# A fused attention and feed-forward kernel: the row maxima of a batch are turned by VectorE in 32x32 blocks instead of by TensorE

## The reference, cut to what matters

```
attn = einsum('bhqd,bhkd->bhqk', q, k) / sqrt(8) + slope[h] * -|i - j|
attn = softmax(attn, axis=-1)
x = layernorm(x + (attn @ v) @ wo.T + bo)
h = silu(x @ w1.T * s1) * (x @ w2.T * s2)
h = gelu(h @ h1.T * s) ; h = gelu(h @ h2.T * s)
x = layernorm(x + h @ w3.T * s3)
```

## Time and profile before

| | us |
|---|---|
| median of 3 runs | 811.47 (810.13 to 813.06) |
| profiled execution | 810.1 |
| its span, first to last instruction | 808.3 |
| busy TensorE / VectorE / ScalarE / GpSimd | 769.6 / 627.9 / 613.5 / 312.0 |

### The profile page before, as it was taken

How to read it: one execution, slowest core, us unless ns; L and a number is a source line. 1 busy time by engine, 2 the same in 40 slices (tenths; PEclk the granted TensorE clock), 3 DMA queues, 4 the chain that set the end, 5 groups by cost and what they waited for, 6 DMA issues and landing times.

```text
span 808.3 us, 26861 instructions
## 1 busy us (share of the span) xinstructions
PE 769.6 (95%) x10370; PEld 557.6 (69%) x10370; DVE 627.9 (78%) x1298; ACT 613.5 (76%) x1099; POOL 312.0 (39%) x488
## 2 busy tenths in 40 slices
PE   3899999999999999999998799999999999999994
PEld 2566666666666666666665578888888888888873
DVE  4789899899989999999993556777777766666764
ACT  3588788788888888888877767777777777777762
POOL 3447878787765657566543200000000000000001
PEclk7599999999999999999999999999999999999997
DMA  6565665656456464564521011111111111101001
GB/s 182 148 176 148 172 187 165 188 152 180 150 172 178 131 172 145 173 173 135 167 66 46 22 34 27 39 40 39 39 39 35 30 39 39 39 26 40 24 16 53
DMA packets 107341, 81.37 MB, mean 101 GB/s; under 512 B 11168, under 2 KB 94112, under 8 KB 107232
## 3 DMA queue, kind: packets, MB, share of 16 engines
q1 hardware_dynamic: 105632, 76.59, 33.3%
q0 software_dynamic: 880, 2.88, 1.3%
q10 hardware_dynamic: 720, 0.36, 0.1%
HBM read 45.72 MB, written 33.55 MB: 98 GB/s over the span
## 4 chain that ended last, share of the span: by engine, by line
PE 91%; DVE 2%; ACT 2%; DMA 2%; issue 1%; POOL 1%; SPq 0%; POOLq 0%; ACTq 0%; DVEq 0%
PE ps_b L947 17%; PE ps_b L950 17%; PE ps_o L524 15%; PE ps_a L465 11%; PE ps_b L473 6%; PE ps_b L580 4%; PE ps_a L950 3%; PE ps_a L947 3%; PE ps_a L549 2%; PE ps_a L480 2%; PE ps_b L541 2%; PE ps_a L563 2%; PE ps_b L480 2%; PE ps_b L571 1%; PE ps_b L535 1%
## 5 line engine op out<-in xcount | busy, mean ns | idle before, releaser
L759 DVE TENSOR_REDUCE neg_sb<-ps_a 128x2 f32<-128x512 f32 x512 | 324.6, 681 | 39.8 <-PE ps_a L480 32.6
L653 ACT ACTIVATE probs<-ps_b 128x512 f32<-128x512 f32 x512 | 281.5, 591 | 57.2 <-PE ps_b L480 57.0
L465 PE MATMUL ps_a<-qk_stack 52*64 52x256 bf16 x2048 | 177.3, 281 | 11.1 <-DMA qk_stack<-qk_scratch 8.2
L473 PE MATMUL ps_b<-qk_stack 54*64 54x256 bf16 x2048 | 172.4, 276 | 1.1 <-ACT probs L653 0.9
L1042 ACT ACTIVATE gelu_f<-ps_b,sc 128x512 f32<-128x512 f32 x128 | 88.3, 690 | 76.3 <-PE ps_b L950 68.7
L465 PEld LDWEIGHTS ps_a<-qk_stack 52*64 52x64 bf16 x2048 | 82.2, 108 | 84.4 <-DVE neg_sb L759 61.4
L524 PE MATMUL ps_o<-probs,v_aug 128*32 128x256 f32 x2048 | 137.5, 385 | 0.0
L1152 POOL TENSOR_SCALAR vareps_f<-meanvar_f 128x4 f32<-128x4 f32 x16 | 9.9, 618 | 319.2 <-DVE meanvar_f L1138 319.2
L480 PE MATMUL ps_a<-corner_sb,eye_sb 64*64 64x128 bf16 x1024 | 116.0, 222 | 0.3 <-issue 0.3
L480 PE MATMUL ps_b<-corner_sb,eye_sb 64*64 64x128 bf16 x1024 | 114.3, 218 | 0.2 <-issue 0.2
L947 PE MATMUL ps_b<-g1h,h_hi 128*128 128x512 f32 x256 | 101.6, 397 | 1.4 <-DVE g1l L1114 1.4
(11 more groups left out here) (112 smaller groups left out, 1429.9 us busy)
## 6 DMA issues: line engine op xcount, KB each, us to landing
qk_stack<-qk_scratch SPq DMA_DIRECT2D x128, 192.0 KB, 3.4
qk_scratch<-qk_sb SPq DMA_DIRECT2D x64, 192.0 KB, 3.0
qk_scratch<-qk_sb SPq DMA_DIRECT2D x96, 128.0 KB, 3.0
xT_sb<-in_xT SPq DMA_DIRECT2D x32, 128.0 KB, 3.5
x_sb<-in_x SPq DMA_DIRECT2D x32, 128.0 KB, 3.5
x_scratch<-x_sb SPq DMA_DIRECT2D x32, 128.0 KB, 3.4
x_in<-x_scratch SPq DMA_DIRECT2D x32, 128.0 KB, 2.1
x_res<-x_scratch SPq DMA_DIRECT2D x32, 128.0 KB, 2.1
```

The costliest lines, as they stand in the source:

```text
L465: pe.matmul(ps[side * TILE:(side + 1) * TILE, qb * SEQ:(qb + 1) * SEQ], q_stack[i][rows_of, j, at:at + TILE], k_stack[i][rows_of, j, :], s ...
L473: pe.matmul(ps[side * TILE:(side + 1) * TILE, kb * SEQ:(kb + 1) * SEQ], k_stack[i][rows_of, j, at:at + TILE], q_stack[i][rows_of, j, :], s ...
L653: nc.scalar.activation(probs[:, h % HALF, :], ps_b[b_bank(t, k)][:], ACT.Exp, scale=slope[h]).then_inc(exp_done, 1)
L759: nc.vector.tensor_reduce(negmax[:, h_a // HALF, h_a % GROUPS, h_a % HALF // GROUPS, :], ps_a[a_bank(t, k)][:].rearrange("p (b k) -> p b k ...
```

## The change

The turn of the maxima goes from TensorE to VectorE, which transposes blocks of 32x32 numbers only. `neg_sb` is now 128x32 (all 16 heads, two blocks of queries each), and `max_f` is 32x128. Behind the reduction of head 15, VectorE waits for all 16 reductions of the batch and writes `max_f` in four instructions, one for each 32 partitions. `turn_max` on TensorE, `copy_max` on ScalarE and their bank uses are gone. GpSimd splits all heads at once, and two transfers lay them in place of four. The first product runs 9 slots ahead in place of 4. In `AT`, `turn norm` goes from slot 8 to 9, `pv 1` from 10 to 9 and `qk` from 13 to 12. On ScalarE the copy of `o_sb` goes from behind slot 3 to behind slot 2 and `copy_oT` from slot 9 to 10. On VectorE `sum_stats` goes from slot 11 to 13.

```diff
-AT = {"v": 1, "wo": 1, "pv 3": 4, "max 0": 6, "turn o": 6, "pv 0": 6, "turn norm": 8, "pv 1": 10, "qk": 13, "max 1": 13, "pv 2": 15}
-AHEAD = 4
+AT = {"v": 1, "wo": 1, "pv 3": 4, "turn o": 6, "pv 0": 6, "turn norm": 9, "pv 1": 9, "qk": 12, "pv 2": 15}
+AHEAD = 9
-B_USES = [... for n in ("v", "max 0", "turn norm", "qk", "max 1") ...]
+B_USES = [... for n in ("v", "turn norm", "qk") ...]
...
-        neg_sb = sb("neg_sb", [P, 2, P])
+        neg_sb = sb("neg_sb", [P, BLK * HEADS])
-        max_f = [sb(f"max_f{i}", [BLK * HALF, P]) for i in range(2)]
+        max_f = sb("max_f", [BLK * HEADS, P])
...
 (SyncE)
-                if live(t, BATCH):
-                    max_rows(t, s, 1)
...
-                if live(t + 1, BATCH) and t >= 0:
-                    max_rows(t + 1, (s + 1) % STACKS, 0)
+                if live(t + 1, BATCH):
+                    max_rows(t + 1, (s + 1) % STACKS)
...
 (TensorE)
-                    if k % HALF == 0:
-                        wait(pe, m_landed[k // HALF], (t + 1) * MPARTS * DMA)
+                    if k == 0:
+                        wait(pe, m_landed, (t + 1) * MPARTS * DMA)
-                    if k == (3 if t < 0 else AT["max 0"]) and live(t + 1, BATCH):
-                        turn_max(t, 0)
-                    if k == AT["max 1"] and live(t + 1, BATCH):
-                        turn_max(t, 1)
...
 (ScalarE)
-                    if k == 3 and live(t - 1, BATCH):
+                    if k == 2 and live(t - 1, BATCH):
                         ...  (copy of o_sb)
-                    if k == 3 and live(t + 1, BATCH):
-                        copy_max(t, 0)
-                    if k == 9 and live(t - 1, BATCH - 1):
+                    if k == 10 and live(t - 1, BATCH - 1):
                         copy_oT(t)
-                    if k == 14 and live(t + 1, BATCH):
-                        copy_max(t, 1)
...
 (VectorE)
+            def turn_max(b):
+                wait(dve, max_done, (b + 1) * HEADS)
+                wait(dve, m_split, b)
+                for n in range(QUADS):
+                    quad = slice(n * SQUARE, (n + 1) * SQUARE)
+                    nc.vector.transpose(max_f[:, quad], neg_sb[quad, :]).then_inc(m_turned, 1)
...
-                        if h_a % HALF == 0:
-                            wait(dve, mT_done, b_a * 2 + h_a // HALF - 1)
+                        if h_a == 0:
+                            wait(dve, m_turned, b_a * QUADS)
                         ...  (the reduction)
+                        if h_a == HEADS - 1:
+                            turn_max(b_a)
-                    if k == 11 and live(t - 2, BATCH):
+                    if k == 13 and live(t - 2, BATCH):
                         sum_stats(t, par)
                     if k == 6 and live(t - 1, BATCH):
                         normalise(t)
...
 (GpSimd)
-                if live(t, BATCH):
-                    split_max(t, 1)
-                if t == -1:
-                    split_max(0, 0)
                 if live(t + 3, BATCH) and t + 3 > 0:
                     split_qk(t + 3, qk_sb[1 - par])
-                if live(t + 1, BATCH) and t >= 0:
-                    split_max(t + 1, 0)
+                if live(t + 1, BATCH):
+                    split_max(t + 1)
```

More of the change, by code:

```diff
@@ L73 @@
 SPILLS = 5
+SQUARE = 32
 XT_BUFS = 6
+QUADS = P // SQUARE
 def slopes():
@@ L93, in wait_apart @@
         eng.sem_inc(passed, 1)
-AT = {"v": 1, "wo": 1, "pv 3": 4, "max 0": 6, "turn o": 6, "pv 0": 6, "turn norm": 8, "pv 1": 10, "qk": 13, "max 1": 13, "pv 2": 15}
-AHEAD = 4
+AT = {"v": 1, "wo": 1, "pv 3": 4, "turn o": 6, "pv 0": 6, "turn norm": 9, "pv 1": 9, "qk": 12, "pv 2": 15}
+AHEAD = 9
 STACKS = 4
 A_USES = [use for k in range(HEADS) for use in (k, *(n for n in ("wo", "turn o") if AT[n] == k))]
-B_USES = [use for k in range(HEADS) for use in (k, *(n for n in ("v", "max 0", "turn norm", "qk", "max 1") if AT[n] == k))]
+B_USES = [use for k in range(HEADS) for use in (k, *(n for n in ("v", "turn norm", "qk") if AT[n] == k))]
 A_BANKS, B_BANKS = 3, 4
@@ L143, in b_batch @@
 def b_batch(t, use):
-    return t + {"v": 0, "max 0": 1, "max 1": 1, "turn norm": -1, "qk": 4}[use] if isinstance(use, str) else t
+    return t + {"v": 0, "turn norm": -1, "qk": 4}[use] if isinstance(use, str) else t
 def last_use(t, use, uses, banks, batch, first):
@@ L270, in attention @@
         xb_sb = [sb(f"xb_sb{i}", [P, BLK, D]) for i in range(2)]
-        neg_sb = sb("neg_sb", [P, 2, P])
-        negmax = neg_sb[:, :, 0:BLK * HALF].rearrange("p n (g h a) -> p n g h a", g=GROUPS, h=HH)
-        max_f = [sb(f"max_f{i}", [BLK * HALF, P]) for i in range(2)]
-        mrow = [sb(f"mrow{i}", [BLK * HALF, MPARTS, P], BF16) for i in range(2)]
+        neg_sb = sb("neg_sb", [P, BLK * HEADS])
+        negmax = neg_sb.rearrange("p (g h a) -> p g h a", g=GROUPS, h=HG)
+        max_f = sb("max_f", [BLK * HEADS, P])
+        mrow = sb("mrow", [BLK * HEADS, MPARTS, P], BF16)
         o_sb = sb("o_sb", [P, 2, SEQ])
@@ L300, in attention @@
         scores_a, max_done = sem("scores_a"), sem("max_done")
-        mT_done, m_copied, m_first, m_split = sem("mT_done"), sem("m_copied"), sem("m_first"), sem("m_split")
-        m_landed = [sem(f"m_landed{i}") for i in range(2)]
+        m_turned, m_first, m_split, m_landed = sem("m_turned"), sem("m_first"), sem("m_split"), sem("m_landed")
         scores_b, exp_done = sem("scores_b"), sem("exp_done")
@@ L308, in attention @@
         bn_done, xb_done = sem("bn_done"), sem("xb_done")
-        neg_set = sem("neg_set")
         ones_set, lo_marked, lo_counted = sem("ones_set"), sem("lo_marked"), sem("lo_counted")
@@ L454, in take_b @@
                         wait(pe, qk_copied, b + 1)
-                    elif isinstance(before[1], str):
-                        wait(pe, m_copied, b * 2 + int(before[1][-1]) + 1)
                     else:
@@ L528, in pv @@
                 mm.then_inc(pv_done, 1)
[L530 to L535, removed]
             def project_v(t):
@@ L625, in _ @@
         def _(act):
[L626 to L629, removed]
-                                     ACT.Copy).then_inc(m_copied, 1)
             def copy_oT(t):
@@ L816, in split_piece, with split_max @@
                 nc.gpsimd.tensor_tensor(lo, raw_piece(n), hi.bitcast(F32), ALU.subtract).then_inc(raw_split, 1)
-            def split_max(b, hf):
-                wait(pool, m_copied, b * 2 + hf + 1)
-                wait(pool, m_landed[hf], b * MPARTS * DMA)
-                nc.gpsimd.tensor_copy(mrow[hf][:, 0, :], max_f[hf][:]).then_inc(m_first, 1)
-                wait(pool, m_first, b * 2 + hf + 1)
-                nc.gpsimd.tensor_tensor(mrow[hf][:, 1, :], max_f[hf][:], mrow[hf][:, 0, :], ALU.subtract).then_inc(m_split, 1)
+            def split_max(b):
+                wait(pool, m_turned, (b + 1) * QUADS)
+                wait(pool, m_landed, b * MPARTS * DMA)
+                nc.gpsimd.tensor_copy(mrow[:, 0, :], max_f[:]).then_inc(m_first, 1)
+                wait(pool, m_first, b + 1)
+                nc.gpsimd.tensor_tensor(mrow[:, 1, :], max_f[:], mrow[:, 0, :], ALU.subtract).then_inc(m_split, 1)
             def split_qk(b, parts):
```

14 lines of the change are left out of this document (5 added, 9 removed).

## The result

The changed kernel takes 888.16 us (887.05 to 889.37, 4 runs), against 812.26 (810.13 to 813.92, 4 runs) for the one before on the same chip. The ratio is 1.0942 [1.0915, 1.0970]: slower by 76 us, where a time of 842 us was predicted, with a range up to 856. The direction was right, the size was not.

What follows compares the result with a forecast made beforehand. TensorE was taken to set the step: 12.64 - 0.49 + 1.01 + 0.52 = 13.67 us. Over the steps, with 2.0 us for the start, that added 30.3 us, giving 842 us; range 824 to 856.

Steps and rivals of the forecast that it cites:

- The step that failed: TensorE's slots: pitch 0.30 then 0.28 us, 0.38 to other work, carried over unchanged to give a 12.15 us step.
- The relief of TensorE: On TensorE, both turns of the maxima (0.37 us) and one interruption of seven (0.12) go: 0.49 us a step.
- TensorE's relief wins: Rival: both new waits together stay below 0.49 us, so the kernel gets faster, 798 us; chance 8%.
- The transposes: Four on VectorE ahead of `normalise`, each in full and the next right behind: 4 x 0.18 = 0.72 us.
- The rival with overlap: VectorE's transposes overlap at 0.08 us each: step 13.27 us, time 831 us; chance 12%.
- The bank wait at slot 9: TensorE waits at slot 9 for the bank that the product of `normalise` on VectorE releases: 1.01 us a step.
- The second wait: On TensorE `qk` waits for `copy_oT`, now behind ScalarE's exponential of slot 10: 0.52 us a step.
- the rival without it: Only the bank wait at slot 9 shows, `copy_oT` being in time: 828 us; chance 5%.
- The maxima rows: Turned, split and transferred rows land by 12.0 us, against a need at slot 0 at 13.67: no wait.
- The start: Five more first products of batch 1 run before the first exponential: +2.0 us, between 0 and 4.
- The case with 67%: The prediction's own forecast: both waits, a step of 13.5 to 14.1 us, 837 to 855 us.
- its four slower cases: Its own forecast (67%) and the rivals at 831 us (12%), 828 us (5%) and 853 us (5%).

Runs made afterwards that it cites:

- halves put right: Changed kernel with the second product of slot k on head k in place of k ^ 1, so a slot's two products have opposite parity: 842.39 us.
- the weight piece moved: Kernel with two transposes, with GpSimd splitting its weight piece ahead of the norm `norm_x1` in place of behind it: 809.67 us, ratio 0.9980.
- the best version: Changed kernel with heads of opposite parity, copy behind slot 9, two transposes behind `normalise`, and GpSimd's weight piece split ahead of `norm_x1`: 809.67 us.
- the kernel with two queues: Kernel with one transpose, GpSimd's weight piece split ahead of `norm_x1`, and four of eight maxima transfers started by ScalarE behind slot 10: 911.77 us.

## Why the prediction was wrong in size

| edit, on the changed kernel | step, us | time, us |
|---|---|---|
| as changed | 15.25 | 888.16 |
| transposes behind `normalise` | 14.51 | 864.97 |
| halves put right | 13.84 | 842.39 |
| and the copy behind slot 9 | 13.26 | 830.67 |
| and the transposes behind `normalise` | 12.88 | 816.07 |
| and two transposes | 12.54 | 815.56 |
| and the weight piece moved | 12.54 | 809.67 |
| the kernel before | 12.64 | 812.26 |

The kernel before was measured again beside each group of runs, with medians from 809.64 to 812.26.

**The step that failed** is "Slots start 0.30 us apart right behind other work, then 0.28, and other work starts 0.38 behind the last slot", carried over to the changed kernel as "If nothing new came up, the step would be 12.15 us". I took a slot's time as a property of its products. It is one of the pair of heads that meet in it. The earlier trace rows had the hint: 313.18 and 313.48, products of `ps_a` and `ps_b` with 52 and 54 rows of the 128, several in flight at a time. The line `g = h % GROUPS` was in the code that I read, but I asked only who waits for whom when `AHEAD` changes, not which heads meet. The missing term measured 1.41 us (15.25 - 13.84). By the starts of the slots in the two traces, four of the six runs of slots end 0.24 to 0.28 us later in the changed kernel. The one that ends at slot 6 ends 0.15 later, as `turn o` behind it has to wait for ScalarE's copy even with the halves right, and the one that ends at slot 9 0.18 later, as it holds the wait for the product. There a part of the loss fell into a wait. The six make up the whole term.

The Trainium skill (TensorEngine Tiling (Array Packing), Key Properties) says that different tiles of the array load and multiply in parallel, and that each tile is tied to its partitions. The trace agrees: 0.00 us between the two purposes in different halves, 0.13 in the same one.

**The relief of TensorE, 0.49 us**: too high by about half, a second term that was wrong. The first turn of the maxima was put at 0.26 and was worth 0.00, since behind slot 6 TensorE waits for the copy of `o_sb` in both kernels. The stretch from slot 7 to slot 11, where two interruptions became one, is 0.10 us shorter in the best version than before (0.12 predicted), and that from slot 11 to the next slot 0 is 0.14 shorter (0.11 predicted). That is 0.24, of which VectorE's delay of `wo` takes 0.14. With four transposes VectorE took 0.3 more at slot 12. The prediction says of slot 9 that the removed work was its cover; it did not ask the same of `turn o`. This is why its rival "TensorE's relief wins" (798) was out of reach.

**The transposes**, taken as 0.72 us with none overlapping: 4 x 0.20 plus three gaps of 0.03 is 0.90 (333.48 to 334.38). The value chosen was low by 0.18, within the bounds of 0.32 and 1.12. That did not lengthen the path to the product, because the first transpose starts 0.08 earlier than predicted and the reciprocal 0.07 ahead of the end of the last one. The rule that was weighed, of the Trainium skill (VectorE: DVE Perf Modes, Two Vector instructions with no wait between them), says that an instruction whose input starts in another group of 32 partitions is held until the earlier ones have finished. Here the trace agrees: they start 0.23 us apart at 0.20 each, while the reciprocal starts 334.31 - 334.18 = 0.13 behind the last one, before its end. No run here has two transposes that start at the same partition, so the trace can't tell this rule from transposes that never overlap. The formula that the same page of the Trainium skill has for fp32 additions (in its section on the TRN2 errata; it is not a table of sizes, as the prediction calls it), (N + 151) cycles at 0.96 GHz, would give 0.19 us by estimate, and the trace has 0.20. The rival with overlap (831) is refuted.

**The bank wait at slot 9**, 1.01 us: place and chain right (1.69 against 1.70 us from reduction to product). With the halves right, slot 9 starts 3.47 us behind slot 6, against the predicted 3.41. But TensorE is ready for it at 2.66 and not at 2.40, since the 0.26 of the removed turn did not go. So the wait is 0.82 us; in the changed kernel moving the transposes gave 0.74 back.

**The second wait**, 0.52: measured 0.53 (13.2 / 25), and 0.58 a step when it was removed (0.21 in steps with a weight piece). So the rival without it (828) is refuted as well.

**The maxima rows**: covered in the changed kernel, as predicted; its list has no wait for them. They came late only with two or one transposes, which bring four or eight transfers.

**The start**, +2 (0 to 4): the first exponential starts at 34.0 us before, at 37.5 in the changed kernel and at 37.1 with the halves put right. So the term is 3.1 to 3.5, within its bounds. In the profiled executions the kernel with the halves right is 32.6 us longer than the one before (840.9 - 808.3): 3.1 in the start, 28.9 from the first exponential of step 0 to that of step 31, and 0.6 behind it.

**The range and the chances**: the one cause outside the list of costs moved the time 32 us above its upper end. The case with 67%, a step of 13.5 to 14.1 us, did not come, nor did any of the rivals. Slower had 88%, and that was right. (Two small slips of the prediction change nothing: its step adds up to 13.68 and not 13.67 us, and its four slower cases to 89% and not 88.)

## What to carry to other kernels

When a constant shifts which items two interleaved streams process at the same time, work out which pairs now meet and whether they share a part of the engine, before carrying over any pitch from the trace. A busy number that rises with fewer instructions is the sign of it: no wait for another engine can do that. And before removed work is counted as gained, look what the next instruction waits for: 0.26 us of the removed work had been filling a wait for another engine. The same look belongs to the engine that takes the work over: it was busy for 12.19 of 12.88 us with 0.7 idle, and still held the other one up in two places.

## What the hardware showed that was not expected

- When the two kinds of products of a slot (52 and 54 rows) have their rows in the same 64 partitions, each run of slots ends 0.27 us later (1.86 / 7, in the kernel before).
- A transpose of 32-number rows takes 0.20 us on VectorE at 32, 64 and 128 partitions alike.
- In two kernels a long wait of TensorE was followed by a lower clock. Two stretches of the kernel with two transposes, the first with a late row (columns as above):

```profile
178.00:180.00 2.00, 0.01 (x2) 0.00 (x0) 1.01 (x2) 0.60 (x2) 1.81 (x4) 1.00 0.08 7
...
181.40:184.80 3.40, 3.40 (x50) 2.43 (x52) 2.56 (x5) 1.28 (x3) 3.31 (x4) 0.51 1.08 211
```

TensorE is busy for 0.01 of 2.00 us, and soon after the granted clock falls to 0.51 (1.2 GHz) for 3.4 us, though it is busy all the time by then. A late row thus cost more than its wait here. In the kernel with two queues:

```profile
303.00:306.00 3.00, 1.05 (x28) 0.51 (x21) 0.62 (x2) 1.13 (x3) 2.91 (x4) 1.00 0.75 150
...
308.00:310.00 2.00, 2.00 (x41) 1.46 (x44) 1.09 (x2) 0.87 (x2) 0.21 (x1) 0.50 0.80 224
```

The same happens there behind a stretch with 1.05 of 3.00 us busy; it is part of what the waits did not explain. The steady stretch of the changed kernel has 1.00 in spite of its two short waits a step.
